# A megakernel's first attention: its three projections from float32 to three f16 products each

## The reference

```python
def _lora(x, W, A, Bm):
    return x @ W.T + x @ Bm.T @ A.T * LORA_S
q = _lora(x, Wq, Aq, Bq)   # likewise k, v; 16 heads of 16
s = jnp.einsum('bhqd,bhkd->bhqk', q, k) / math.sqrt(DH)
s = s + alibi[None] + mask
p = jax.nn.softmax(s, axis=-1)
o = jnp.einsum('bhqk,bhkd->bhqd', p, v)
return o @ Wp.T            # added to x; the input of the layer is layernorm(x)
```

## Time and profile before

| | us |
|---|---|
| three runs | 2403.80, 2404.24, 2404.24 |
| median | 2404.24 |
| the profiled execution | 2399.85 |
| its span, first to last instruction | 2398.0 |
| L0 attention in it, from the first transposes to the last addition to x | 29.96 to 657.3 |

### The profile page before, as it was taken

The page is one execution under the profiler, slowest core; times in us unless marked ns, Lnnn a source line. Parts: engine busy times, 40 slices in busy tenths (PEclk is TensorE's granted clock), DMA queues, the critical chain, the costliest instruction groups (busy, mean ns, idle before and its releaser), DMA issues. The chain is left out here.

```text
span 2398.0 us, 56553 instructions
## 1 busy us (share of the span) xinstructions
PE 2014.5 (84%) x18246; PEld 1457.5 (61%) x18247; DVE 1731.8 (72%) x3603; ACT 1470.1 (61%) x2926; POOL 1032.3 (43%) x1226
## 2 busy tenths in 40 slices
PE   3999999999862997487898989989898999739999
PEld 2766766666561665155666767666666767525665
DVE  3877777777792443477687777869597886579997
ACT  1867766677562444186677676858587787434443
POOL 4534533345004000589655465747465574032222
PEclk8999999999956999699999999999999999959999
DMA  6000000000033332012100000000000000100000
GB/s 232 2 2 0 0 0 0 0 0 1 2 118 131 104 86 74 4 15 36 15 2 3 2 3 2 2 2 2 3 2 3 2 2 2 37 1 13 15 17 25
DMA packets 53114, 57.64 MB, mean 24 GB/s; under 512 B 7120, under 2 KB 47216, under 8 KB 52896
## 3 DMA queue, kind: packets, MB, share of 16 engines
q1 hardware_dynamic: 46240, 45.00, 6.1%
q0 software_dynamic: 6656, 9.85, 2.0%
HBM read 36.22 MB, written 18.61 MB: 23 GB/s over the span
## 5 line engine op out<-in xcount | busy, mean ns | idle before, releaser
L1028 ACT ACTIVATE prob_sb<-a_bank,neg_max_sb 128x128 f32<-128x128 f32 (+3 forms) x512 | 256.5, 529 | 159.7 <-DVE neg_max_sb L1107 146.6
L1107 DVE TENSOR_REDUCE neg_max_sb<-a_bank 128x1 f32<-128x128 f32 (+3 forms) x512 | 237.2, 486 | 142.2 <-PE a_bank L896 135.9
L371 PE MATMUL a_bank<-w_in_sb,xnT_sb 128*128 128x512 f16 x1152 | 293.4, 393 | 29.0 <-DVE t_buf_sb L579 20.6
L531 DVE TENSOR_REDUCE neg_max_sb<-a_bank 128x1 f32<-128x128 f32 (+3 forms) x512 | 235.7, 481 | 110.7 <-PE a_bank L288 109.9
L434 ACT ACTIVATE prob_sb<-a_bank,neg_max_sb 128x128 f32<-128x128 f32 (+3 forms) x512 | 259.1, 537 | 57.6 <-DVE neg_max_sb L531 54.8
L442 ACT ACTIVATE p_hi_sb<-a_bank 128x384 f16<-128x384 f32 (+1 forms) x384 | 204.5, 533 | 116.3 <-PE a_bank L297 115.2
L538 DVE TENSOR_TENSOR p_lo_sb<-a_bank,p_hi_sb 128x384 f16<-128x384 f32 (+1 forms) x384 | 227.6, 594 | 52.7 <-ACT p_hi_sb L442 50.4
L453 ACT ACTIVATE stack_sb<-a_bank 128x1024 f16<-128x1024 f16 (+1 forms) x256 | 209.7, 820 | 45.1 <-PE a_bank L342 43.4
L297 PE MATMUL a_bank<-ident_f_sb,prob_sb 128*128 128x128 f32 x1280 | 208.2, 278 | 0.6 <-ACT prob_sb L434 0.6
L707 POOL TENSOR_TENSOR rope_w_sb<-t_buf_sb,sin_sb 128x256 f32<-128x256 f32 x128 | 125.0, 976 | 185.5 <-DVE t_buf_sb L579 183.6
L909 PE MATMUL a_bank<-ident_f_sb,prob_sb 128*128 128x128 f32 x1280 | 204.4, 274 | 0.1
(11 more groups left out here) (253 smaller groups left out, 5524.3 us busy)
## 6 DMA issues: line engine op xcount, KB each, us to landing
sorted_rows<-zeros_sb SPq DMA_DIRECT2D x1, 4992.0 KB, 21.8
x_in_sb<-sorted_rows SPq DMA_DIRECT2D x39, 128.0 KB, 2.2
sorted_results<-y_moe_sb SPq DMA_DIRECT2D x39, 128.0 KB, 1.7
x_sb_sb<-L_attn_x SPq DMA_DIRECT2D x8, 512.0 KB, 10.7
w_raw_sb<-L_ffn_gate_bank SPq DMA_DIRECT2D x8, 512.0 KB, 4.1
w_raw_sb<-L_ffn_up_bank SPq DMA_DIRECT2D x8, 512.0 KB, 5.0
w_raw_sb<-L_ffn_down_bank SPq DMA_DIRECT2D x8, 512.0 KB, 6.3
out<-x_sb_sb SPq DMA_DIRECT2D x32, 128.0 KB, 1.7
```

The lines of the kernel that those rows point to most:

```text
L371: last = pe.matmul(out, xnT[:, x, c, j * P:(j + 1) * P], w["in"][:, w_, c, cols], start=k == 0, stop=k == len(terms) - 1)
L531: last = dve.tensor_reduce(neg_max[:, i:i + 1], S[(3 * h + g) % 2][:, off:off + L], AX.X, ALU.max, negate=True)
L1028: last = act.activation(prob[g][:, h % 2, off:off + L], S[(3 * h + g) % 2][:, off:off + L], ACT.Exp, bias=neg_max[:, i:i + 1])
L1107: last = dve.tensor_reduce(neg_max[:, i:i + 1], S[(3 * h + g) % 2][:, off:off + L], AX.X, ALU.max, negate=True)
```

## The change

The projections' operands are split in a high f16 part and a low f16 part, the difference between the value and its high part, and the product is the sum of high x high, high x low and low x high in one PSUM group. The weights are split once, scaled by 16, after the fold; the takers of the products divide by 16. x's and y's transposes are split as they leave PSUM: ScalarE writes the high part, VectorE subtracts it from PSUM and writes the low part, and it is VectorE's subtraction that now frees the bank.

```diff
+    TERMS = [(a, b, c) for a, b in ((0, 0), (0, 1), (1, 0)) for c in range(C)]
-    xnT = sb("xnT0", [P, C, T], F32)
+    xnT = sb("xnT0", [P, 2, C, T], F16)
-    yT = sb("yT0", [P, CHUNKS, T], F32)
+    yT = sb("yT0", [P, 2, CHUNKS, T], F16)
...
-                for c in range(C):
-                    last = pe.matmul(out[:, 0:256], xnT[:, c, j * P:(j + 1) * P], w["in"][:, c, half * 384:half * 384 + 256],
-                                     start=c == 0, stop=c == C - 1)
+                for n, (x_, w_, c) in enumerate(TERMS):
+                    last = pe.matmul(out[:, 0:256], xnT[:, x_, c, j * P:(j + 1) * P],
+                                     w["in"][:, w_, c, half * 384:half * 384 + 256],
+                                     start=n == 0, stop=n == len(TERMS) - 1)
...
-                act.activation(xnT[:, :, j * P:(j + 1) * P],
-                               W[bank][:, 0:D].rearrange("p (c n) -> p c n", c=C), ACT.Copy).then_inc(s_xnT, 1)
+                act.activation(xnT[:, 0, :, j * P:(j + 1) * P],
+                               W[bank][:, 0:D].rearrange("p (c n) -> p c n", c=C), ACT.Copy).then_inc(s_xnTh, 1)
...
-                act.activation(yT[:, c, :], W[bank][:, :], ACT.Copy).then_inc(s_yT, 1)
+                act.activation(yT[:, 0, c, :], W[bank][:, :], ACT.Copy).then_inc(s_yTh, 1)
...
+            elif kind == "xT":
+                j, = a
+                wait(dve, s_xnTh, b * QT + j + 1)
+                dve.tensor_tensor(xnT[:, 1, :, j * P:(j + 1) * P], W[bank][:, 0:D].rearrange("p (c n) -> p c n", c=C),
+                                  xnT[:, 0, :, j * P:(j + 1) * P], ALU.subtract).then_inc(s_xnT, 1)
+            elif kind == "yT":
+                c, = a
+                wait(dve, s_yTh, b * CHUNKS + c + 1)
+                dve.tensor_tensor(yT[:, 1, c, :], W[bank][:, :], yT[:, 0, c, :], ALU.subtract).then_inc(s_yT, 1)
...
-                dve.tensor_tensor(x_sb[:, bass.ds(tile, 1), :].rearrange("p o d -> p (o d)"),
-                                  x_sb[:, bass.ds(tile, 1), :].rearrange("p o d -> p (o d)"),
-                                  W[bank][:, 0:D], ALU.add).then_inc(s_proj, 1)
+                x_tile = x_sb[:, bass.ds(tile, 1), :].rearrange("p o d -> p (o d)")
+                dve.scalar_tensor_tensor(out=x_tile, in0=W[bank][:, 0:D], scalar=1.0 / W0_SCALE, in1=x_tile,
+                                         op0=ALU.mult, op1=ALU.add).then_inc(s_proj, 1)
...
+                    for n, (raw_, parts_) in enumerate(((w_out_raw, w_out), (w_raw, w_in))):
+                        dve.wait_ge(s_high, n + 1)
+                        dve.scalar_tensor_tensor(out=parts_[:, 1, :, :], in0=raw_[:, :, :], scalar=W0_SCALE,
+                                                 in1=parts_[:, 0, :, :], op0=ALU.mult, op1=ALU.subtract)
+
+                @block.scalar
+                def _(act):
+                    act.wait_ge(s_w, 160)
+                    act.activation(w_out[:, 0, :, :], w_out_raw[:, :, :], ACT.Copy, scale=W0_SCALE).then_inc(s_high, 1)
+                    act.wait_ge(s_fold, 8)
+                    act.activation(w_in[:, 0, :, :], w_raw[:, :, :], ACT.Copy, scale=W0_SCALE).then_inc(s_high, 1)
```

More of the change, by code:

```diff
@@ L30 @@
 TERMS0 = 6 * DH0
+W0_SCALE = 16.0
 K0 = TERMS0 + 6
@@ L962, in fill @@
                 j, = a
[L963 to L966, removed]
+                for n, (x_, w_, c) in enumerate(TERMS):
+                    last = pe.matmul(out[:, 0:256].rearrange("p (f n) -> p f n", f=2), xnT[:, x_, c, j * P:(j + 1) * P],
+                                     w["in"][:, w_, c, :].rearrange("p (f n) -> p f n", f=2)[:, :, 256:384],
+                                     start=n == 0, stop=n == len(TERMS) - 1)
                 taken[bank] = (s_v, QT, off, j + 1)
@@ L982, in fill @@
                 wait(pe, s_yT, (b + 1) * CHUNKS)
-                for c in range(CHUNKS):
-                    last = pe.matmul(out[:, 0:D], yT[:, c, i * P:(i + 1) * P], w["out"][:, c, :],
-                                     start=c == 0, stop=c == CHUNKS - 1)
+                for n, (y_, w_, c) in enumerate(TERMS):
+                    last = pe.matmul(out[:, 0:D], yT[:, y_, c, i * P:(i + 1) * P], w["out"][:, w_, c, :],
+                                     start=n == 0, stop=n == len(TERMS) - 1)
                 taken[bank] = (s_proj, QT, off, i + 1)
@@ L1062, in take @@
                 act.activation(parts[:, p % 2, :, 0, :],
[L1063 removed]
+                               W[bank][:, 0:256].rearrange("p (h d) -> p h d", d=DH), ACT.Copy,
+                               scale=1.0 / W0_SCALE).then_inc(s_ph, 1)
             elif kind == "values":
@@ L1131, in take @@
                 dve.wait_ge(s_ph, m + 1)
-                dve.tensor_tensor(rest[:, p % 2, :, :], W[bank][:, 0:256].rearrange("p (h d) -> p h d", d=DH),
-                                  parts[:, p % 2, :, 0, :], ALU.subtract).then_inc(s_taken, 1)
+                dve.scalar_tensor_tensor(out=rest[:, p % 2, :, :], in0=W[bank][:, 0:256].rearrange("p (h d) -> p h d", d=DH),
+                                         scalar=1.0 / W0_SCALE, in1=parts[:, p % 2, :, 0, :],
+                                         op0=ALU.mult, op1=ALU.subtract).then_inc(s_taken, 1)
+            elif kind == "xT":
[7 more added lines that the diff above has]
+                dve.tensor_tensor(yT[:, 1, c, :], W[bank][:, :], yT[:, 0, c, :], ALU.subtract).then_inc(s_yT, 1)
             elif kind == "oT":
@@ L2224, in build @@
             banks = [scope.enter_context(nc.psum_tensor(f"a0_bank{i}", [P, 512], F32)) for i in range(8)]
-            w_in = psb("w_in0", [P, C, 3 * D], F32)
-            w_out = psb("w_out0", [P, C, D], F32)
+            w_raw = psb("w_raw0", [P, C, 3 * D], F32)
+            w_out_raw = psb("w_out_raw0", [P, C, D], F32)
+            w_in = psb("w_in0", [P, 2, C, 3 * D], F16)
+            w_out = psb("w_out0", [P, 2, C, D], F16)
+            s_high = sem("l0_weights_high_ready")
             zeros = psb("zeros", [P, 2 * D], F16)
```

12 lines of the change are left out of this document (7 added, 5 removed).

## The result

The change was forecast at 2412.0 us, slower, and came out faster: 2393.11 us (median of 6, 2390.89 to 2395.20) against 2403.14 us before (median of 6, 2400.04 to 2404.24), a ratio of 0.9961 with a 95% interval of 0.9949 to 0.9973. The profiled execution of after has a span of 2389.1 us, that of before 2398.0.

A forecast was written before the change was run, and what follows sets the result against it. No single bound: TensorE, VectorE and ScalarE all near three quarters busy or above, with stops between them. 3.35 + 3.3 + 6 x 0.05 + 0.4 + 0.5 = 7.85 us on 2404.24 gave 2412.0; range 2403 to 2416.

The forecast's parts named there:

- Rival A: TensorE sets the pace throughout the L0 attention stage: 2384 us with all its saving, 2398 with half; chance 0.11 together.
- Weights, +3.35: Before the L0 attention stage, ScalarE and VectorE split w_in and w_out with nothing hiding it: 3.35 us more.
- Prologue, +3.3: Start of L0 attention: normalizing, transposing and splitting tiles becomes a serial chain, so the first piece comes later: 3.3 us more.
- A steady batch, +0.05: One middle batch of L0 attention, slots k = 0 to 47: TensorE's 3.4 us gain and VectorE's 3.1 us work nearly cancel.
- The low part of yT: Slot k = 18 of a batch: VectorE's 0.69 us subtraction makes the maximum late and takes back some 0.3 us.
- The bank at k = 24: Transposes of xT tile 1 wait for VectorE to free tile 0's bank; the 0.6 to 0.7 us lead falls to about 0.
- The low part of k = 42: Late in a batch, VectorE's 0.69 us yT subtraction makes the next maxima slip 0.6 us, mostly covered by GpSimd's 0.95 wait.
- Gain of a fill: Each TensorE projection fill falls from 0.86 to 0.65 us: 0.21 saved, 16 fills, 3.4 us a batch.
- First and last batch, and the end, +0.9: L0 attention's outer batches: first +0.2, last +0.2; at the end yT's low part is bare before the proj fills, +0.5 us.

## Why the prediction was wrong

Its sum was for the stage, and the stage kept to it. What failed is its last sentence: "What comes after the stage isn't touched." No instruction behind the stage was touched, but their places in TensorE's program were, and that was worth 15.9 us in the traces, twice the whole sum: the term that the prediction put at nothing was the cost of fetching the L1 loop's next block at five turns back, 3.2 us each. With the head put back to where the kernel before has it, the changed kernel takes 2409.56 us against 2403.75, +5.8, near the +7.8 of the forecast; the two pairs of like heads give +7.5 and +6.7. No rival covered it. Rival A had the right side and a wrong mechanism: TensorE's saving was there, 2.25 us a batch when alone, but VectorE's work took it back. That the kernel came out faster is luck: of where the loop's head lay before, and of where 192 more instructions put it.

Step by step:

- **Weights, +3.35:** 3.2 (30.56 against 27.34 in the earlier trace rows). Right, each duration within 0.02 us.
- **Prologue, +3.3:** 3.0 (the first stack 6.2 us later in all). The first piece was taken by ScalarE at 41.12, forecast 41.6. The prediction gives 1.2 GHz as the granted clock of the transposes at 29.96. No row shows that: the windows of this stretch read 1.00, though two transposes are recorded over 0.69 us where the earlier trace rows has 0.39. The 0.73 us that it took from the rows held all the same.
- **A steady batch, +0.05:** 0.00, and its walk held where it could be seen. In a batch's trace the scores are earlier by 0.9 us against its own beginning at k = 17 to 19, and by 0.5 at k = 24, where 0.6 to 0.7 was said. The low part of yT takes back 0.5 by k = 20 (forecast 0.3). The bank at k = 24 costs 0.66 in the scores of k = 25 (0.6 to 0.7). The low part of k = 42 makes the scores of k = 45 0.93 later, of which 0.54 returns at k = 46 (0.6 was forecast for the maxima, most of it covered). But the sum hid its two large terms. The windows of the earlier trace rows couldn't tell "both engines have slack" from "neither has, and they cancel"; the pair of half changes could.
- **Gain of a fill:** sixteen fills gave 2.25 us a batch of the 3.4 counted, so two thirds of it lies on the path when VectorE doesn't stand in the way.
- **First and last batch, and the end, +0.9:** the profiled executions show 2.8. The last four proj fills ran below full clock in after (24 matmuls in 4.45 us) and at full clock in the changed kernel with its head at slot 0 (2.95), though the stage is the same code. Before is no steadier: 3.69 us for its 16, and 6.71 with the head at slot 0. So a microsecond or two of this term belong to the execution, not to the change; the medians of the pairs, 6.7 and 7.5, hold the sum of 7.85 to about 1 us, and closer with the microsecond of the MoE's loop.

The windows show it: in before's last fills the granted clock was 1.00,

```profile
652.00:655.00 3.00, 2.31 (x11) 2.08 (x12) 1.14 (x3) 0.54 (x1) 0.00 (x0) 1.00 0.00 0
```

and 0.50 in the kernel that differs from it only in the place of L1's loop:

```profile
652.00:655.00 3.00, 2.69 (x6) 2.19 (x7) 0.57 (x2) 0.17 (x1) 0.00 (x0) 0.50 0.00 0
```

Could the profile have warned? Yes: the waits of before listed eleven microseconds at L342 released by nothing, at the same spot behind each turn back. That is a cost that depends on where the code lies. A change that adds some 200 instructions ahead of it was bound to move it, though from the trace alone one could not have said to a better or to an equal place with much confidence. With the stop 17 instructions behind the head, though, the slot 239 and the count of 192 could have been worked out, and would have given a rival near 2396.

What stays open: why the granted clock falls behind some stops and not others, why a turn of the MoE's loop is 0.06 us shorter with the moved code, and whether the 3 us to the next block's arrival hold for other engines; no run looked at these.

## What to carry to other kernels

Before costing a change, look in the waits for stops that nothing releases, at the same spot of every turn of a loop: they belong to the place of the code, and any edit ahead of them, however unrelated, may move or remove them; compare kernels with the loop heads held at the same slot, or else an edit's own effect (+7 us here) is read with the opposite sign. For a loop whose head is fetched again at each turn, the start (slot 0) and the middle (128) of a block were the best places tried here. And when a walk through a loop ends at zero, measure its two halves apart: zero may be two large terms, and then moving one of them to an engine with room (here 2393.81 to 2377.76 us with its prologue) is the real gain.

## What the runs showed of the hardware

- A turn back of TensorE's loop of 2805 instructions fetches 16384 bytes of instructions and stops its matmuls for 2.3 to 3.1 us; that of its loop of 1431 instructions fetches nothing and doesn't stop.
- The next block comes 2.8 to 3.4 us after the turn's first matmul. So a head 17 to 20 slots short of a block's end costs another 1.9 to 2.7 us, 48 slots short 0.5 to 1.6, 81 slots short 0.4 or 0.8 at one turn of five, and 128 or 256 nothing.
- With the head at slots 236 and 239 the granted clock is 0.50 for 6.8 us behind every turn back. With no second stop it is so for 3.4 us behind most, and for 6.8 us or not at all behind a few.
- 96 unused matmuls far ahead moved the loop's head by 192 slots and made the kernel 13.2 us faster.
- Announcing the loop's branch removes the stop at the turn back, but adds 3.05 us at the exit.
- GpSimd split 128x256 values into high and low f16 in 0.61 + 0.67 us from SBUF, where ScalarE and VectorE need 0.38 + 0.42 from PSUM; 9.6 us more of it in a batch did not slow VectorE (56.85 us busy, as without).
